# Attention with a ternary feed-forward on one core: output products turned into split three-pass ones, with a new order of the units around them

## The reference, cut to what matters

```python
xn = layernorm(x)
q, k, v = split_heads(xn @ Wq), split_heads(xn @ Wk), split_heads(xn @ Wv)
w = softmax(q @ k.T / 64 + causal)
w = w * clip((key_no + span_val * 1024) / 33, 0, 1)
w = w / (sum(w) + 1e-8)
attn = merge_heads(w @ v) @ Wo                 # Wo: 1024 x 128
ffn = dequantised(round(clip(xn / scale))) @ (ternary - 1).T + bias
out = x + attn + ffn
```

## Time and profile before

| | |
|---|---|
| median of 3 runs | 1000.46 us (1000.36 to 1007.18) |
| the profiled execution's own time | 1000.45 us |
| its span, first to last instruction | 998.7 us |
| PE busy, share of the span | 98% |
| DVE, POOL, ACT busy | 76%, 71%, 45% |
| granted TensorE clock | 1.000 of full speed throughout |

### The profile page before, as it was taken

One profiled execution on the slowest core, in us unless ns is written; L12 is line 12 of the kernel. 1 busy time (PEld: TensorE's weight loads), 2 busy tenths in 40 slices (PEclk: granted clock), 3 DMA queues, 4 the chain that ended last, 5 costly groups with the idle time before them and its releaser, 6 DMA issues.

```text
span 998.7 us, 19217 instructions
## 1 busy us (share of the span) xinstructions
PE 983.3 (98%) x7125; PEld 633.6 (63%) x7125; DVE 756.3 (76%) x1706; ACT 451.4 (45%) x607; POOL 706.4 (71%) x649
## 2 busy tenths in 40 slices
PE   8999999999999999999999999999999999999997
PEld 4565666666666666666666666666666666666654
DVE  7877888878788878787767777777777667777754
ACT  4444445444444444454443454443454444454442
POOL 8766767767767667867766767667767667777672
PEclk9999999999999999999999999999999999999999
DMA  6000000000000000000000000000000000000000
GB/s 177 3 2 2 2 1 3 2 3 2 2 22 3 2 2 2 1 2 2 2 12 13 1 3 2 2 2 3 1 2 23 3 2 2 1 3 2 2 2 22
DMA packets 16133, 8.52 MB, mean 9 GB/s; under 512 B 5404, under 2 KB 15644, under 8 KB 16040
## 3 DMA queue, kind: packets, MB, share of 16 engines
q1 hardware_dynamic: 15416, 7.15, 2.6%
q10 hardware_dynamic: 624, 0.14, 0.1%
HBM read 4.33 MB, written 2.10 MB: 6 GB/s over the span
## 4 chain that ended last, share of the span: by engine, by line
PE 86%; DVE 9%; issue 2%; POOL 1%; ACT 1%; DMA 1%; DVEq 0%; SPq 0%; ACTq 0%; POOLq 0%
PE pv L1025 25%; PE ring L1008 23%; PE ring L970 12%; PE beside L1067 7%; PE beside L1040 6%; DVE ring L770 3%; PE ring L943 3%; PE ring L939 3%; PE ring L940 3%; DVE v L757 3%; DVE beside L794 1%; PE beside L1055 1%; PE beside L977 1%; PE ring L957 1%; PE ring L958 0%
## 5 line engine op out<-in xcount | busy, mean ns | idle before, releaser
L569 ACT ACTIVATE prob<-ring 128x1024 f32<-128x1024 f32 (+3 forms) x384 | 293.6, 810 | 346.7 <-PE ring L1008 346.6
L503 POOL TENSOR_TENSOR psumd<-psumd,prob 128x512 f32<-128x512 f32 (+1 forms) x250 | 406.2, 1625 | 28.9 <-POOL psumd L503 1.3
L770 DVE CUSTOM_DVE_ANT_0 ring<-ring,causal 128x128 f32<-128x128 f32 (+3 forms) x512 | 240.4, 517 | 97.1 <-PE ring L970 96.3
L1008 PE MATMUL ring<-q,k 64*128 64x512 f32 (+3 forms) x2304 | 279.8, 347 | 2.3 <-DMA mrow<-maxrow 0.8
L1025 PE MATMUL pv<-prob,v 128*64 128x512 f32 (+3 forms) x1536 | 267.1, 490 | 0.0
L476 POOL TENSOR_SCALAR_AFFINE_SELECT prob<-prob 128x256 f32<-128x256 f32 x256 | 109.4, 429 | 217.0 <-ACT prob L569 214.9
L1008 PEld LDWEIGHTS ring<-q,k 64*128 64x128 f32 x2304 | 194.6, 185 | 37.6 <-DVE rowmax L770 5.2
L1025 PEld LDWEIGHTS pv<-prob,v 128*64 128x64 f32 x1536 | 104.9, 137 | 154.1 <-issue 142.0
L774 DVE TENSOR_REDUCE rowmax<-ring 128x2 f32<-128x1024 f32 x128 | 151.4, 1222 | 3.9 <-PE ring L970 0.5
L499 POOL TENSOR_TENSOR psumd<-prob 128x768 f32<-128x768 f32 (+1 forms) x63 | 132.5, 2103 | 24.2 <-ACT prob L569 19.1
L970 PE MATMUL ring<-k,q 64*128 64x512 f32 (+3 forms) x768 | 142.9, 408 | 3.0 <-DVE k L746 0.7
(11 more groups left out here) (120 smaller groups left out, 943.3 us busy)
## 6 DMA issues: line engine op xcount, KB each, us to landing
kext<-kext SPq DMA_DIRECT2D x128, 4.0 KB, 1.7
out<-x_sb SPq DMA_DIRECT2D x8, 256.0 KB, 2.4
x_sb<-in_L_attn_query SPq DMA_DIRECT2D x3, 512.0 KB, 5.5
mrow<-maxrow SPq DMA_DIRECT2D x62, 4.0 KB
x_sb<-in_L_attn_query SPq DMA_DIRECT2D x2, 256.0 KB, 4.3
xn_sb<-in_L_attn_Wv SPq DMA_DIRECT2D x1, 512.0 KB, 5.2
wo<-in_L_attn_Wo SPq DMA_DIRECT2D x1, 512.0 KB, 7.0
xn_sb<-in_L_attn_Wq SPq DMA_DIRECT2D x1, 448.0 KB, 3.5
```

The source lines that it names most:

```text
L503: g.tensor_tensor(acc[:, :, lo:HALF], acc[:, :, lo:HALF], pr[:, :, lo:HALF], ALU.add).then_inc(acc_done, 1)
L569: a.activation(prob[n % NPROB][:, :, lo:HALF], ring[:, slot(f"S{t}", i), :, lo:HALF], ACT.Exp, scale=1.0 / DH).then_inc(exp_done, 1)
L770: last = v.tensor_tensor_reduce(out=ring[:, s, h, 0:n], in0=ring[:, s, h, 0:n], in1=causal[:, HALF - n:HALF], scale=1.0, scalar=MASKED, op ...
L1008: last = t_.matmul(ring[:, s, h, lo:HALF], k[p][rows, keys], q[p][rows, cols], start=(at == 0), stop=(at == len(parts) - 1))
```

## The change

1. Pairs 0 to 30: the output product becomes three one-pass products of 512 columns. `wo` is split once into `wo1` and `wo2` (ACT and POOL, in pair 0). ACT writes the high part of the scaled values (`h`, 128x512) and DVE the rest (`l`, 128x512, two inputs in SBUF). Weights are now the rows of Wo and the values stream, so the result comes out turned: columns of the output on the partitions.
2. The turned result is summed in `yt` (128x1024) over a batch's pairs. In the second pair of the next batch it is turned back by eight transposes in two units P0 and P1 on PE, which DVE adds to `x_sb`. The last pair keeps plain fp32 products; P0 and P1 of the last batch stand in it.
3. The feed-forward product of the first three batches becomes one fp32 matmul of 512 columns for each half.
4. Order on PE: Y0 goes from behind M9 to behind the next pair's K; D0 and G3 from behind S7 to in front of M6; Y1 from behind M5 to behind M8; X and W from in front of G11 to behind it. DVE and ACT follow: t0 and u0 now come in front of R6 and R7, E7 behind ln0 and ex0, and Ya1 and Ya0 move with their products.
5. Memory: `xn_sb` shrinks from four batches to three, and the first third is `yt` (and holds Wo while it is split). The logarithms are written into `r0`. There is one `o_sb` for both halves. The fourth batch is normalised at pairs 16 and 17 (was 11 and 12), the bias of batch 3 is added at pair 18 (was 14), and a quantising step falls on the last seven pairs of a batch (was the first seven).

```diff
-PE_PLAN = ("T Q+ K+ X0 X1 W G11- M0+ M1+ S0 S1 S2 M2+ D1- M3+ S3 V+ S4 S5 M4+ S6 M5+ Y1- M6+ M7+ S7 D0 G3 "
-           "M8+ S8 S9 S10 M9+ Y0 M10+ M11+ S11 G7")
-ACT_PLAN = "Z Qhi+ Khi+ X0 X1 E0 E1 E2 ln1- ex1- E3 E4 E5 E6 E7 ln0 ex0 E8 E9 E10 E11"
-DVE_PLAN = ("Tc Z Qlo+ Klo+ R0+ R1+ X0 X1 W R2+ R3+ t1- u1- Vs+ o1- R4+ R5+ Ya1- R6+ R7+ t0 u0 R8+ o0 q "
-            "R9+ R10+ Ya0 R11+")
-POOL_PLAN = "L0 A0 L1 A1 L2 A2 L3 A3 B0 A4 A5 A6 A7 L8 L9 L10 L11 A8 A9 A10 A11 B"
+PE_PLAN = ("T Q+ K+ P0 Y0- G11- P1 X0 X1 W M0+ M1+ S0 S1 S2 M2+ D1- M3+ S3 V+ S4 S5 M4+ S6 M5+ D0 G3 M6+ S7 M7+ "
+           "M8+ Y1- S8 S9 S10 M9+ M10+ M11+ S11 G7")
+ACT_PLAN = "Z Qhi+ Khi+ X0 X1 wo E0 E1 E2 ln1- ex1- E3 E4 E5 E6 h1- ln0 ex0 E7 E8 E9 E10 E11 h0"
+DVE_PLAN = ("Tc Z Qlo+ P0 Ya0- Klo+ P1 R0+ R1+ X0 X1 W R2+ R3+ t1- u1- Vs+ o1- R4+ R5+ l1- t0 u0 R6+ R7+ o0 "
+            "R8+ Ya1- q R9+ R10+ R11+ l0")
+POOL_PLAN = "L0 A0 L1 A1 L2 A2 L3 A3 B0 A4 A5 A6 A7 L8 L9 L10 L11 A8 A9 A10 A11 B wo"
...
-PE_LAST = "T G11- S0 S1 S2 D1- S3 S4 S5 S6 Y1- S7 D0 G3 S8 S9 S10 S11 Y0 D1 F1 G7 G11 Y1"
+PE_LAST = "T G11- S0 S1 S2 Y0- D1- S3 S4 P0 S5 S6 Y1- S7 D0 G3 S8 S9 P1 S10 S11 Y0 D1 F1 G7 G11 Y1"
 POOL_LAST = "L0 A0 L1 A1 L2 A2 L3 A3 L8 L9 L10 L11"
-DVE_LAST = "Tc t1- u1- o1- A5 Ya1- A6 A7 t0 u0 o0 A8 A9 Ya0 t1 u1 o1 Ya1"
-SP_PLAN = "mrow kext+ store-"
+DVE_LAST = "Tc q Ya0- t1- u1- o1- P0 A5 l1- A6 Ya1- A7 t0 u0 o0 P1 A8 A9 Ya0 t1 u1 o1 Ya1"
+ACT_LAST = "E0 E1 E2 ln1- ex1- E3 E4 h1- E5 E6 E7 ln0 ex0 E8 E9 E10 E11"
+SP_PLAN = "mrow kext+ wl store--"
...
+    if name in ("P0", "P1"):
+        return i == LAST or i % PAIRS_OF_BATCH == 1 and i > PAIRS_OF_BATCH
...
+                elif name == "wo":
+                    pool.wait_ge(wo_hi_done, 1)
+                    g.tensor_tensor(wo2[:, :, :].rearrange("p n d -> p (n d)"), yt,
+                                    wo1[:, :, :].rearrange("p n d -> p (n d)").bitcast(F32), ALU.subtract
+                                    ).then_inc(wo_lo_done, 1)
...
+            def values_high(i, c):
+
+                act.wait_ge(o_done, halves_upto(i, c))
+                if halves_upto(i, c) > 1:
+                    act.wait_ge(y_ready, halves_upto(i, c) - 1)
+                a.activation(o_hi[:, :], o_sb[:, :], ACT.Copy).then_inc(o_hi_done, 1)
...
+            def values_low(i, c):
+
+                dve.wait_ge(o_hi_done, halves_upto(i, c))
+                v.tensor_tensor(o_lo[:, :], o_sb[:, :], o_hi[:, :].bitcast(F32), ALU.subtract
+                                ).then_inc(o_lo_done, 1)
...
             def add_output(i, c):
 
-                b = i // NPB
                 dve.wait_ge(y_ready, halves_upto(i, c))
+                cols = slice(c * HALF, (c + 1) * HALF)
+                if i == LAST:
+                    ins = add_rows(B - 1, c)
+                elif i % NPB == 0:
+                    if i == 0:
+                        dve.wait_ge(wo_lo_done, 1)
+                    ins = v.tensor_copy(yt[:, cols], beside[:, :])
+                else:
+                    ins = v.tensor_tensor(yt[:, cols], yt[:, cols], beside[:, :], ALU.add)
+                ins.then_inc(y_added, 1)
+
+            def add_turned_back(i, c):
+
+                b = batch_turned_back(i)
+                dve.wait_ge(turned_back, 2 * b + c + 1)
                 dve.wait_ge(bias_added, b + 1)
...
+                add_rows(b, c).then_inc(rows_added, 1)
...
+                elif unit[0] == "P":
+                    pe.wait_ge(rows_added, 2 * batch_turned_back(j) + int(unit[1:]) + 1)
...
+            def turn_back(i, c):
+
+                b = batch_turned_back(i)
+                pe.wait_ge(y_added, halves_upto(min(b * NPB + NPB - 1, LAST - 1), c))
+                for k in range(HB):
+                    n = c * HB + k
+                    last = t_.transpose(beside[:, k * P:(k + 1) * P], yt[:, n * P:(n + 1) * P], ident[:, :])
+                last.then_inc(turned_back, 1)
+
             def feed_forward(i, c):
...
+                if i < LAST:
+                    t_.matmul(beside[:, :], ternT[:, :], fq[:, c * HALF:(c + 1) * HALF], start=True, stop=False)
+                    return
...
             def output_projection(i, c):
...
-                pe.wait_ge(o_done, halves_upto(i, c))
-                for k in range(HB):
-                    last = t_.matmul(beside[:, k * P:(k + 1) * P], o_sb[c][:, k * P:(k + 1) * P],
-                                     wo[:, i % NPB, :], start=not with_ffn, stop=(not with_ffn or k == HB - 1))
+                if i < LAST:
+                    if i == 0 and c == 0:
+                        pe.wait_ge(wo_lo_done, 1)
+                    pe.wait_ge(o_hi_done, halves_upto(i, c))
+                    w_hi, w_lo = wo1[:, i % NPB, :], wo2[:, i % NPB, :]
+                    t_.matmul(beside[:, :], w_hi, o_hi[:, :], start=not with_ffn, stop=False)
+                    t_.matmul(beside[:, :], w_lo, o_hi[:, :], start=False, stop=False)
+                    pe.wait_ge(o_lo_done, halves_upto(i, c))
+                    last = t_.matmul(beside[:, :], w_hi, o_lo[:, :], start=False, stop=True)
```

More of the change, by code:

```diff
@@ L97, in walk @@
     seen = set()
-    for i in range(-1, N_PAIRS + 1):
+    for i in range(-1, N_PAIRS + 2):
         for word in (first if i < 0 else plan if last is None or i < LAST else last).split():
@@ L111 @@
 IN_RING = [("X", -2)] + [u for u in PE_ORDER if u[0][0] in "QKSMV" or u == ("D1", LAST)]
-IN_BESIDE = [u for u in PE_ORDER if u[0][0] in "THDYXWF" and u not in (("D1", LAST), ("Y1", LAST))]
+IN_BESIDE = [u for u in PE_ORDER if u[0][0] in "THDYXWFP" and u not in (("D1", LAST), ("Y1", LAST))]
 PLACE = {u: n for n, u in enumerate(IN_RING)}
@@ L382, in _ @@
                     place_key_weights(i, i % 2)
+                elif name == "wl":
+                    sp.wait_ge(tern_done, 1)
+                    sp.dma_start(wo_last, wo_dram[(NPB - 1) * P:NPB * P, :]).then_inc(wo_last_landed, 16)
                 else:
                     b = i // NPB
[L385 to L388, removed]
+                    for c in range(2):
+                        if i == LAST:
+                            sp.wait_ge(y_added, halves_upto(i, c))
+                        else:
+                            sp.wait_ge(rows_added, 2 * b + c + 1)
+                        store(b, c * HB, (c + 1) * HB)
             sp.wait_ge(out_stored, 16 * 2 * B)
@@ L596, in _ @@
                 turned_high(0, c, ring[:, slot("X", -2), c, :])
-            for name, i in walk(ACT_PLAN, ACT_FIRST):
+            for name, i in walk(ACT_PLAN, ACT_FIRST, ACT_LAST):
                 if name in ("Qhi", "Khi"):
@@ L693, in quantise @@
             def quantise(b, step):
-                over = xn_sb[:, b * S:(b + 1) * S].bitcast(U32)
+                over = xn_sb[:, (XN_AT[b] or 2) * S:((XN_AT[b] or 2) + 1) * S].bitcast(U32)
                 if b or step > 1:
@@ L922, in turn @@
                 for k in range(HB):
-                    n = b * KB + c * HB + k
-                    last = t_.transpose(out[:, k * P:(k + 1) * P], xn_sb[:, n * P:(n + 1) * P], ident[:, :])
+                    n = c * HB + k
+                    last = t_.transpose(out[:, k * P:(k + 1) * P], xn_rows(b, n), ident[:, :])
                 last.then_inc(turned_ready, 1)
@@ L1060, in output_projection @@
                 with_ffn = i % NPB == NPB - 1
-                if i == 0 and c == 0:
-                    pe.wait_ge(wo_landed, 16)
                 if with_ffn and (f"F{c}", i) not in PLACE_BESIDE:
                     feed_forward(i, c)
-                pe.wait_ge(o_done, halves_upto(i, c))
-                for k in range(HB):
-                    last = t_.matmul(beside[:, k * P:(k + 1) * P], o_sb[c][:, k * P:(k + 1) * P],
-                                     wo[:, i % NPB, :], start=not with_ffn, stop=(not with_ffn or k == HB - 1))
+                if i < LAST:
[7 more added lines that the diff above has]
+                    last = t_.matmul(beside[:, :], w_hi, o_lo[:, :], start=False, stop=True)
+                else:
+                    pe.wait_ge(wo_last_landed, 16)
+                    pe.wait_ge(o_done, halves_upto(i, c))
+                    for k in range(HB):
+                        last = t_.matmul(beside[:, k * P:(k + 1) * P], o_sb[:, k * P:(k + 1) * P],
+                                         wo_last, start=not with_ffn, stop=(not with_ffn or k == HB - 1))
                 last.then_inc(y_ready, 1)
@@ L1103, in _ @@
                     idle_products(2 * P)
+                elif name[0] == "P":
+                    turn_back(i, int(name[1:]))
                 elif name[0] == "F":
```

77 lines of the change are left out of this document (58 added, 19 removed).

## The result

The changed kernel takes **1048.68 us** (median of 4 runs, 1046.78 to 1054.8) against 1000.5 us for the kernel before on the same chip: ratio 1.0485, 95% interval 1.0456 to 1.0514, 4.9% slower. The prediction said 1024.0 us, 1000 to 1034: the right sign, half of the size. The profiled execution took 1049.19 us, its span is 1047.5 us, so 1.7 us lie around the span, as before.

A forecast was written before the change was run, and what follows sets the result against it. The prediction took PE, busy for 98% of the span, as the bound. Plain pairs +12, splitting Wo +3.4, turning back +7 and the rest +1 sum to 23.4 on 1000.45: 1024 us, range 1000 to 1034.

The forecast's parts named there:

- Part 1: Output products: three passes cost 0.70 us a half instead of 1.09, taking 24 us off PE over 62 halves.
- Part 2: Y0 behind the next pair's K: covers no wait, costs its full 0.70 us a pair; Ya0 on DVE stays hidden.
- Part 3: D0 and G3 before M6, Y1 behind M8: M8 waits 0.55 us for R6; +0.1 us a pair.
- Part 4: Nothing between M9 and M10: about 0.7 us of Y0's 1.09 turns into a wait; -0.4 us a pair.
- Part 5: DVE's subtractions l beside POOL's adds: held by the port but hidden, 0 us a pair (bounds 0 to 0.2).
- neither cover held: Rival, chance 0.18: the wait at M8 or M11 is smaller than counted; 1008 us without M8's, 1003 without M11's.
- PE didn't stay the bound: Rival that PE stays the bound, chance 0.14: both waits, at M8 and M11, go; 987 us.
- the port: Rival, chance 0.03: POOL's next add starts ahead of l1 in each pair, t0 slips 2.4 us; 1098 us.
- the split saves nothing: Rival, chance 0.03: the three passes of an output product cost 1.09 us after all; 1048 us.
- Part 6: Splitting Wo: PE waits once for POOL's part before Y0 of pair 0; +3.4 us (bounds 2 and 4.5).
- Part 7: Turning back in pairs 9, 17 and 25: Y0 waits for P0's add, P1 adds transposes; +7 us (bounds 4 and 10).
- The rest, +1: Feed-forward product, quantising steps, last pair's P0 and P1, moved X, taken together: +1 us (bounds -2 and +4).

The follow-up runs named there:

- Experiment 2: The changed kernel with only Y1 moved on PE from behind M8 to in front of it; 1034.49 us, ratio 1.0335.
- experiment 3: The changed kernel without DVE's subtraction l, the third pass streaming the high part again; 1048.34 us, ratio 1.0475.
- experiment 4: The kernel before with plain fp32 output products and only the new order of units, nothing split or turned back; 1033.58 us, ratio 1.0343.
- experiment 1: The changed kernel with POOL's part of splitting Wo moved from the end of pair 0 to right behind the bias step; 1043.47 us, ratio 1.0423.
- experiment 10: The changed kernel with Wo split early, Y1 before M8, Y0 between M9 and M10, P0 behind Q, last pair reordered, quantising on first seven pairs; 995.87 us.

## Why the prediction was half wrong

**Part 1 (the products), mis-sized.** Its "it costs 3 x 0.23 = 0.70 us, since Q and K are the same shape and format" holds only in a row of such passes. Behind K it did (757.97, 758.20, 758.43). Between the products of 64 rows it is 0.90. The first and the last pass are the longer ones, at the borders between 64 and 128 rows. The trace of the kernel before had such a border already, in V, whose passes of 128 rows and 256 columns follow a product of 64 rows (timeline of PE, the pair of the earlier trace rows):

```profile
612.56 0.39 PE L957 MATMUL ring<-wv,x 128*128 128x256 f32 x1
612.79 0.28 PE L958 MATMUL ring<-wv,x 128*128 128x256 f32 x1
612.90 0.29 PE L959 MATMUL ring<-wv,x 128*128 128x256 f32 x1
```

From start to start the first pass takes 0.23 us and the second 0.11. The plain product's 1.09 was read between neighbours of 64 rows and holds its borders; the 0.70 set against it holds none. The Trainium skill, page "TensorEngine Tiling (Array Packing)", section "Key Properties", says that changing the tiling mode drains TensorE. The trace agrees in that each border costs 0.10 to 0.11 us; that it is the drain, and not something else in the change of form, was not tried alone.

**Part 2 (Y0 behind K) was right:** first S of the pair 6.40 us behind T instead of 5.72, +0.68 against +0.70, and DVE did hide Ya0.

**Part 3 is the step that failed in a plain pair, in its last term: the price of Y1 behind M8.** Its chain was right: M8 came 5.54 us after M5, where the text's starts give 5.59 (D0 began as placed, h1 took 0.62 instead of 0.6). The term behind it, 0.16 plus Y1's 0.70 from M8 to S8, measured 1.16 instead of 0.86: 0.20 is the dearer product, and 0.10 is M8 itself, which starts behind a wait (776.37 to 776.63 is 0.26, not 0.16). With 0.05 less in front, M5 to S8 grew by 0.37 and not by 0.1. Experiment 2 shows the remedy, the product in front of the waiting unit.

**Part 4 (nothing between M9 and M10) was right:** M9 to S11 1.52 against 1.5, M10 released by ACT, in 31 pairs 9.7 us. Two small pieces complete the missing 0.4 a pair: S8 to M9 +0.06 and S11 to T +0.08, with the 0.27 of Part 3.

**Part 5 (l) was right** in a plain pair: experiment 3, 0.01. In the last pair it wasn't zero: Y1's third pass waits 1.39 us for l1. **The rivals** fell with it: neither cover held (1003 and 1008), PE didn't stay the bound (987), the port cost nothing in the plain pairs (1098). The last rival, "the split saves nothing", named 1048, and that is the time, but by luck. Its mechanism was three passes as dear as the plain product's 1.09; they took 0.69 behind K and 0.90 elsewhere, and the split saved 0.3 a pair against experiment 4.

**Part 6 (Wo), 6.0 instead of 3.4 (5.45 of it went with experiment 1), and Part 7 (turning back), 11.0 instead of 7.** In both the wait was sized nearly right (3.51; 2.56 instead of 2.1), and what came behind it was left out: a lower clock for some microseconds, 1.7 us at the first and, in one of two equal cases, 1.3 at the second. Of the 4 us more in turning back, the clock is 1.3 and the longer waits 1.1; the rest was not traced.

**The rest, +1, was the other failed step.** It held the last pair with "P0 and P1 stand once in the last pair, mostly under a chain that runs through POOL". The last pair grew by 7.0. Its timeline of PE answers to the earlier trace rows, with a line of stretches below:

```profile
1011.62 1.08 PE L1131 MATMUL beside<-psumd,ones 128*64 128x512 f32 x4 [0.78 <-DVE xn_sb L893]
...
1015.53 0.66 PE L1147 MATMUL beside<-ident,xn_sb 128*128 128x128 f32 x4 [1.24 <-DVE rden L861]
...
1020.29 0.50 PE L1174 MATMUL beside<-o_lo,wo 128*128 128x512 f32 x1 [1.39 <-DVE o_lo L874]
...
1022.02 1.93 PE L1131 MATMUL beside<-psumd,ones 128*64 128x512 f32 x4
```

```profile
1010.00:1025.00 15.00, 11.50 (x62) 5.72 (x64) 8.24 (x10) 8.13 (x12) 6.07 (x8) 0.90 0.00 1
```

D1 waits for Ya0, since both need the bank `beside`; P0 waits for u1 for the same reason; Y1's third pass waits for l1, which DVE does behind its first addition of `psumd`; and at a lower clock D0 took 1.93 instead of 1.08 and G3 behind it 3.22 instead of 2.32. This last term comes and goes: in the profiled execution of experiment 1, whose last pair has the same plans, D0 and G3 had their usual lengths, and the stretch from the G7 of pair 30 to the end is 44.45 instead of 46.97. The waits were to be read from the plans: the bank is handed from unit to unit in order, and the last pair has few ring products between them. The 25 us by which the forecast fell short (48.8 on the span against 23.4) are thus 12 in the plain pairs, 2.6 in pair 1, 4 in turning back and about 6 in the last pair. The range was too narrow as well: the upper bounds that the prediction names add up to about 1042, not 1034, and even that is short of 1048.68.

## What to carry to other kernels

A short unit is worth most as a cover: put it in front of the instruction that waits, never behind it, and never where nothing waits; here two products taken out of their covers cost 33 us by order alone (experiment 4). Take the price of a new form from a row with the same neighbours as it will have, not only the same shape. And add to each wait of some microseconds on PE what the clock may take from the work behind it.

## What the runs showed of the hardware

After a stand of 3.51 us PE's mean granted clock was 0.66 over the next 5.0 us, and 16 matmuls took 4.07 us instead of 2.37; with the stand gone in experiment 1 they took 2.37. After two stands of 1.96 us (pairs 9 and 17) the clock fell in one case and not in the other, in one execution; in that of experiment 1 it was 0.66 over 5.0 us behind the stand of pair 9 too.

The times of single runs go with their mean granted clock: the changed kernel took 1046.78 us at 0.996, 1048.18 and 1049.19 at 0.994 and 1054.8 at 0.986, while experiment 10, at 0.998 to 1.000, stayed within 2.7 us. The stands may be where the lower clocks come from, but not alone: the kernel before has no such stand and once took 1006.98 at 0.990.

A pass of 512 columns with 128 rows took 0.23 us from start to start among its like and 0.33 to 0.34 at the borders to products with 64 rows.
